# Layer norm and last logits of the second half moved behind the first gather list, shifts and products of ones put into waits, in a gated recurrence, long filter and mixture-of-experts kernel

## The reference, cut to what matters

```python
x = layernorm(h).reshape(-1, D)
gate_logits = x @ gate_weight.T                      # 16 experts
top_vals, top_idx = jax.lax.top_k(gate_logits, 2)
mask = any(top_idx[:, :, None] == arange(E), axis=1)
hs = silu(einsum('td,efd->tef', x, w1))
h_mean = einsum('tef,te->ef', hs, mask) / maximum(counts, 1)[:, None]
y_mean = einsum('ef,edf->ed', h_mean, w2)
out = einsum('tk,tkd->td', softmax(top_vals), y_mean[top_idx])
```

## Time and profile before

| | |
|---|---|
| time, median of 3 runs | 421.78 us (421.72 to 421.83) |
| span of the profiled execution | 501.4 us |
| the profiled execution's own time | the page gives none beside the span |
| instructions | 7310 |
| TensorE busy | 397.6 us, 79% |
| VectorE busy | 311.4 us, 62% |
| ScalarE busy | 218.1 us, 43% |
| GpSimd busy | 205.3 us, 41% |
| granted TensorE clock, mean | 0.877 |
| front, to the last added filter output | 0 to 158.7 us |
| routing | 158.7 to 252.0 us |
| experts | 252.0 to 467.6 us |
| tail | 467.6 to 501.4 us |

### The profile page before, as it was taken

How to read it: one execution, slowest core, us unless ns; L and a number is a source line. 1 busy time by engine, 2 the same in 40 slices (tenths; PEclk the granted TensorE clock), 3 DMA queues, 4 the chain that set the end, 5 groups by cost and what they waited for, 6 DMA issues and landing times.

```text
span 501.4 us, 7310 instructions
## 1 busy us (share of the span) xinstructions
PE 397.6 (79%) x1929; PEld 269.9 (54%) x1930; DVE 311.4 (62%) x827; ACT 218.1 (43%) x423; POOL 205.3 (41%) x231
## 2 busy tenths in 40 slices
PE   8999999998898987554591404589987877899984
PEld 7888888886898974423440101244433433344552
DVE  3598888888788999543530101577744543577884
ACT  3334555445232666536350101456644443567320
POOL 2011111115400998757467775400066666610510
PEclk9999999998998996756587556799999788999998
DMA  6206533322209350647312111100291111100029
GB/s 182 66 1 164 139 86 109 102 80 82 81 1 262 98 140 2 193 140 212 106 57 52 54 52 43 31 0 2 54 331 47 37 47 42 47 16 1 1 73 251
DMA packets 53020, 43.68 MB, mean 87 GB/s; under 512 B 20686, under 2 KB 45980, under 8 KB 52732
## 3 DMA queue, kind: packets, MB, share of 16 engines
q1 hardware_dynamic: 44276, 32.09, 22.3%
q0 software_dynamic: 4416, 9.05, 6.5%
q10 hardware_dynamic: 4296, 2.15, 1.6%
HBM read 34.86 MB, written 8.42 MB: 86 GB/s over the span
## 4 chain that ended last, share of the span: by engine, by line
PE 47%; DVE 19%; issue 12%; another core or an unknown queue 10%; ACT 6%; POOL 3%; DVEq 2%; ACTq 0%; POOLq 0%
PE P L662 16%; PE P L935 14%; PE P L867 6%; ACT P L1265 4%; DVE BIG L1712 3%; DVE H L1828 2%; PE P L905 2%; PE P L1062 2%; PE P L697 2%; PE P L655 1%; POOL XN L597 1%; DVE arena L1504 1%; POOL arena L594 1%; PE P L688 1%
## 5 line engine op out<-in xcount | busy, mean ns | idle before, releaser
L1712 DVE TENSOR_TENSOR BIG<-BIG,P 128x512 f32 x138 | 95.0, 688 | 115.9 <-issue 75.1
L935 PE MATMUL P<-w1T,arena 128*128 x276 | 142.4, 652 | 12.0 <-DVE BIG L1712 8.7
L935 PEld LDWEIGHTS P<-w1T,arena 128*128 128x128 f32 x276 | 52.6, 209 | 67.1 <-issue 66.4
L1254 ACT COPY arena<-P 128x384 f32<-128x384 f32 (+1 forms) x48 | 22.4, 467 | 119.6 <-remote 50.4
L1265 ACT ACTIVATE P<-P 128x512 f32<-128x512 f32 x138 | 72.8, 580 | 1.6 <-PE P L935 1.5
L614 POOL DMA_INDIRECT XN<-table,arena x60 | 58.1, 968 | 30.1 <-issue 18.1
L614 POOL DMA_INDIRECT arena<-table,arena x42 | 39.7, 946 | 57.9 <-PE P L935 40.8
L557 POOL TENSOR_TENSOR rs<-ve,mhalf 123x4 f32<-123x4 f32 x16 | 17.6, 1098 | 101.9 <-DVE ve L1356 101.9
L1103 ACT ACTIVATE arena<-P 128x492 f32<-128x492 f32 x48 | 27.9, 583 | 50.6 <-PE P L662 50.5
L614 POOL DMA_INDIRECT BIG<-table,arena x36 | 34.6, 960 | 24.7 <-remote 12.4
L905 PE MATMUL P<-ident,XN 128*128 128x128 f32 x60 | 11.4, 304 | 41.6 <-issue 35.3
(11 more groups left out here) (242 smaller groups left out, 639.7 us busy)
## 6 DMA issues: line engine op xcount, KB each, us to landing
arena<-kpad SPq DMA_DIRECT2D x16, 492.0 KB, 4.0
XN<-in_L_ffn_w SPq DMA_DIRECT2D x1, 4096.0 KB
arena<-in_x SPq DMA_DIRECT2D x16, 224.0 KB
table<-XN SPq DMA_DIRECT2D x4, 896.0 KB
BIG<-table SPq DMA_DIRECT2D x1, 2048.0 KB
out<-H SPq DMA_DIRECT2D x8, 224.0 KB
out<-H ACTq DMA_DIRECT2D x8, 224.0 KB
BIG<-table SPq DMA_DIRECT2D x1, 1024.0 KB
```

The source lines that it names most:

```text
L935: mm = nc.tensor.matmul(bank[:, :], stat, w1T[:, bass.ds(e * FF, FF)], start=True, stop=True)
L1254: nc.scalar.copy(GTs[:, bank, 0:count * SLOT], PT[:, 0:count * SLOT]).then_inc(GT_ready, 1)
L1712: v.tensor_tensor(at, at, bank[:, :], ALU.add).then_inc(esum_step, 1)
```

## The change

- Statistics of quarters 2 and 3, their moments and shifts, go from in and around the first two searches to `top2(2)` and behind `top2(3)`. Shifts 0 and 1 are made between steps of `top2(0)`.
- Only 13 of the 16 tiles of logits stand before the first list; the last three, and five w1 groups instead of six, stand behind it on TensorE and ScalarE.
- `ranks(3)` stands ahead of `pick_transposes(2)` and w1 10 and 11; `tile_experts(2)` ahead of w1 12 to 15.
- The powers of quarters 2 and 3 stand in the stream of gathers, ahead of numbers 7 and 19. GpSimd norms 8 sequences of quarters 0 and 1 only, VectorE 6 of quarter 3, ScalarE the rest: 4 of quarter 1 and all 16 of quarter 2 between steps of the one-hots, 10 of quarter 3 behind the last w1 copy.
- 89 products of ones (`stay_warm`), of 256 columns in quarters 0 and 1 and 512 in 2 and 3, stand ahead of TensorE's waits. Their results are not read.

```diff
-NORM_POOL = (8, 8, 8, 0)
+NORM_POOL = (8, 8, 0, 0)
+NORM_DVE = (0, 0, 0, 6)
+X2_FIRST = 13
+        RSTD_AT = (7, 19)
...
             clear(7, 8, 16)
             write_table(2)
             clear(11, 0, 4)
-            write_table(3)
             clear(13, 4, 6)
             clear(15, 6, 8)
+            write_table(3)
...
-            norms(0)
+            rstd_of(0)
...
+            rstd_of(1)
+            norms(0)
             norms(1)
-            norms(2)
-            norms(3)
...
+                    if n in RSTD_AT:
+                        rstd_of(QA + RSTD_AT.index(n))
                     if n in paces:
                         pool.wait_ge(*paces[n])
                     gather(n, g)
...
+            def stay_warm(n, wide=False):
+
+                place = P[1][:, :] if wide else P[3][:, 256:512]
+                cols = oneb[:].unsqueeze(1).to_broadcast([128, 4 if wide else 2, 128])
+                for _ in range(n):
+                    nc.tensor.matmul(place, oneb[:], cols, start=True, stop=True)
...
             def ranks(q):
+                stay_warm((0, 4, 2, 1)[q], q >= 2)
...
             def picks(q):
+                    if n == ON_ACT - OG:
+                        stay_warm(3 if q < 2 else 1, q >= 2)
...
             def bit_transposes(q):
+                stay_warm((5, 6, 8, 4)[q], q >= 2)
             def matches(q):
+                stay_warm((4, 3, 1, 5)[q], q >= 2)
...
+                    if a == 2 and q == 0:
+                        tile_base(1)
+                    if a == 2 and q != 2:
+                        stay_warm(3 if q == 3 else 5, q == 3)
...
             def pick_transposes(q):
+                stay_warm(2 if q >= 2 else 4, q >= 2)
...
...
-            for n in range(2 * NHB):
+            for n in range(X2_FIRST):
                 x2_transposes(n)
-                if n == 11:
+                if n == 10:
                     ranks(0)
...
-            for m in range(0, 2):
-                w1_transposes(m)
             bit_transposes(0)
-            tile_base(1)
...
             tile_experts(1, NA)
-            for m in range(2, 8):
+            for n in range(X2_FIRST, 2 * NHB):
+                x2_transposes(n)
+                if n > X2_FIRST:
+                    logits(n - 1)
+            logits(2 * NHB - 1)
+            for m in range(0, 5):
                 w1_transposes(m)
             ranks(2)
-            for m in range(8, 10):
+            for m in range(5, 10):
                 w1_transposes(m)
             bit_transposes(2)
             matches(2)
             picks(2)
+            ranks(3)
             pick_transposes(2)
             for m in range(10, 12):
                 w1_transposes(m)
-            ranks(3)
...
             picks(3)
             pick_transposes(3)
+            tile_experts(2, NB)
             for m in range(12, E):
                 w1_transposes(m)
...
             copy_V(0)
+            for b in NORM_ACT[1][4:]:
+                norm2(b)
...
             for m in range(12, E):
                 copy_w1T(m)
+            for b in NORM_ACT[3]:
+                norm2(b)
             copy_of(0)
...
-            top2(2, nothing)
+            top2(2, more_stats(2))
...
             counts(2)
+            moments2(2)
             experts_of_tiles(1, 0, NA)
...
             top2(3, between)
             counts(3)
+            for b in range(3 * QB, 3 * QB + 6):
+                bn(b)
             places(3)
             placed(2)
             low_onehots(3, 0)
+            for b in range(3 * QB + 6, 4 * QB):
+                bn(b)
+            moments2(3)
...
+            shift(3)
             experts_of_tiles(2, NA, NB)
             placed(3)
+            for b in range(4 * QB - NORM_DVE[3], 4 * QB):
+                a = v.tensor_scalar(XN[0:T, b], H[0:T, b], mm2[0:T, 0, b:b + 1], rs2[0:T, b:b + 1],
+                                    ALU.subtract, ALU.mult)
+            a.then_inc(xn2_dve, 1)
             index_list(2, P[7], NA, NB)
```

More of the change, by code:

```diff
@@ L43 @@
 QW = QB * E
-NORM_POOL = (8, 8, 8, 0)
-NORM_ACT = [list(range(q * QB, (q + 1) * QB - NORM_POOL[q])) for q in range(NQ)]
+NORM_POOL = (8, 8, 0, 0)
+NORM_DVE = (0, 0, 0, 6)
+NORM_ACT = [list(range(q * QB, (q + 1) * QB - NORM_POOL[q] - NORM_DVE[q])) for q in range(NQ)]
 NCHUNK = 2 * NQ
+X2_FIRST = 13
 SLOT = 128
@@ L302, in build @@
         W1_AT, MATCH_AT = {}, {}
-        at_ring = 2 * NHB
-        for part, q in ((range(0, 2), 0), ((), 1), (range(2, 10), 2), (range(10, 12), 3)):
+        X2_AT = list(range(X2_FIRST))
+        at_ring = X2_FIRST
+        for part, q in (((), 0), ((), 1), (range(0, 10), 2), (range(10, 12), 3)):
+            if q == 2:
+                X2_AT += range(at_ring, at_ring + 2 * NHB - X2_FIRST)
+                at_ring += 2 * NHB - X2_FIRST
             for m in part:
@@ L589, in _, with rstd_of @@
             nc.gpsimd.tensor_scalar(rankb[:], rank_in, 1.0, None, ALU.mult).then_inc(pool_const, 1)
-            def norms(g):
+            def rstd_of(g):
                 pool.wait_ge(ve2_ready, g + 1)
@@ L594, in norms @@
                 nc.gpsimd.tensor_tensor(rs2[0:T, qb], ve2[0:T, qb], mhalf[0:T], ALU.pow).then_inc(rstd2, 1)
+            def norms(g):
                 pool.wait_ge(rstd2, g + 1)
@@ L709, in x2_transposes @@
             def x2_transposes(n):
-                if n >= 2:
-                    pe.wait_ge(ring_read, n - 1)
+                at = X2_AT[n]
+                if at >= 2:
+                    pe.wait_ge(ring_read, at - 1)
                 for q in range(4):
-                    mm = nc.tensor.transpose(PR[n % 2][:, q * T:(q + 1) * T], H[0:T, 4 * n + q], ident[0:T, 0:T])
+                    mm = nc.tensor.transpose(PR[at % 2][:, q * T:(q + 1) * T], H[0:T, 4 * n + q], ident[0:T, 0:T])
                 mm.then_inc(ring_mm, 1)
@@ L882, in tile_base @@
             def tile_base(nth):
+                if nth == 2:
+                    stay_warm(4, True)
                 pe.wait_ge(tiles_ready, nth)
@@ L962, in _ @@
             totals(1, 2 * QA)
-            logits(2 * NHB - 1)
+            logits(X2_FIRST - 1)
             pe.wait_ge(match_ok, 1)
-            for m in range(0, 2):
-                w1_transposes(m)
             bit_transposes(0)
-            tile_base(1)
             matches(0)
@@ L1232, in _ @@
                 copy_x2T(n)
-            for n in range(12, 16):
-                if n == 14:
-                    code_OH(0)
-                for b in NORM_ACT[1][2 * (n - 12):2 * (n - 11)]:
-                    norm2(b)
-                copy_x2T(n)
+            copy_x2T(12)
+            code_OH(0)
+            for b in NORM_ACT[1][:4]:
+                norm2(b)
             code_OH(1)
-            for m in range(0, 2):
-                copy_w1T(m)
             copy_bits(0)
@@ L1247, in _ @@
             copy_V(1)
-            for b in NORM_ACT[2]:
-                norm2(b)
-            for m in range(2, 8):
+            for n in range(X2_FIRST, 2 * NHB):
+                copy_x2T(n)
+            for m in range(0, 5):
                 copy_w1T(m)
@@ L1278, in silus_past @@
                         nc.scalar.copy(xh[:, h, 0:4 * T], PRT[:, 0:4 * T]).then_inc(RT_high, 1)
-            for b in NORM_ACT[3][:6]:
-                norm2(b)
             code_OH(2)
-            for m in range(8, 10):
+            for m in range(5, 10):
                 copy_w1T(m)
@@ L1287, in _ @@
             low_onehots(2)
+            for b in NORM_ACT[2][:2]:
+                norm2(b)
             copy_V(2)
+            code_OH(3)
             for m in range(10, 12):
                 copy_w1T(m)
-            for b in NORM_ACT[3][6:]:
-                norm2(b)
-            code_OH(3)
             copy_bits(3)
             low_onehots(3)
+            for b in NORM_ACT[2][2:8]:
+                norm2(b)
             copy_V(3)
+            for b in NORM_ACT[2][8:]:
+                norm2(b)
             for m in range(12, E):
                 copy_w1T(m)
+            for b in NORM_ACT[3]:
+                norm2(b)
             copy_of(0)
@@ L1622, in _ @@
             moments2(1)
-            shift(0)
             def more_stats(g):
@@ L1630, in more_stats, with shifts @@
                 return between
-            top2(0, more_stats(2))
-            for b in range(2 * QB + (4 * 11 + 2) // 3, 3 * QB):
-                bn(b)
-            counts(0)
-            moments2(2)
-            shift(1)
+            def shifts(i):
+                if i in (2, 8):
+                    shift(i // 8)
+            top2(0, shifts)
             def tile_counts(nth):
@@ L1722, in add_tile, with count_first @@
                 accumulate(n, expert_bank(n), n)
-            top2(1, more_stats(3))
-            for b in range(3 * QB + (4 * 11 + 2) // 3, 4 * QB):
-                bn(b)
+            def count_first(i):
+                if i == 2:
+                    counts(0)
+            top2(1, count_first)
             counts(1)
-            moments2(3)
             places(0)
@@ L1733, in _ @@
```

(11 more changed lines are left out.)

17 lines of the change are left out of this document (12 added, 5 removed).

## The result

The changed kernel takes **427.47 us** (median of 4 runs, 426.4 to 428.0) against 421.75 for the kernel before: a ratio of **1.0141, 95% interval 1.0127 to 1.0155**. It is slower by 5.7 us. The forecast was 419.1 in a range up to 424.0, so it missed in sign and in size. The mechanism of case D, a late gather 32, is what happened; its price was put at 1.9 to 3.2.

The account below looks back on a forecast made before the run. Without holds, TensorE's products and the gathers were taken to bound the kernel equally within 1 us. TensorE's chain gains 5.0, the gathers' 2.7 if the runs have the 4.6 us hold: 421.78 - 2.7 = 419.1 us, range 415.0 to 424.0.

Parts of the forecast that it names:

- case D: Rival, slower: the power ahead of gather 19 makes gather 32 late; +1.9, up to +3.2 us, 423.7; chance 0.31.
- 246.0: GpSimd, kernel before: start of gather 32 if the runs too have the 4.6 us hold in VectorE's routing work.
- 243.3: GpSimd, changed kernel: start of gather 32, last moments at 223.9 plus 19.4 for the second power and thirteen gathers.
- VectorE and TensorE up to the lists: Routing stage: first list 4.1 us earlier, quarter 3's counts 6.2 earlier, first expert product 3.2 earlier, at 238.0.
- Number 32 waits for the second list: GpSimd, kernel before: gather 32 starts only once the second list is there, at 252.21 in the profile.
- 241.4: GpSimd, kernel before: start of gather 32 with the holds taken out of the profiled 252.21.
- About 3.5 us lost that nobody waits for: GpSimd's gather stream: the first power, ahead of gather 7, loses about 3.5 us at no cost to the end.
- 237.1, then 1 to issue and 4 to land: 242: SyncE: second table write, behind ScalarE's last norm at 237.1, lands at 242, when gather 32 may start.
- A: Forecast chosen: the gathers set the end and start 2.7 us earlier, 419.1 us; chance 0.32.
- the equality of the two chains: Expert stage, kernel before: TensorE's products and the gathers end within 1 us of each other, so both must be shortened.
- 415.8: Kernel before: span in us without holds, 501.4 less 74.8, 6.2 and 4.6; the median was 421.78.
- B: Rival: TensorE sets the end and gathers keep up, needing an interval under about 1.17 us; -5.0 us, 416.8; chance 0.20.

Follow-up runs that it names:

- split wait: Changed kernel, table writes of quarters 2 and 3 on semaphores of their own, gather 32 waiting for quarter 2's alone, 42 for quarter 3's: 424.43 us, 1.0077 to before.
- the profiled TensorE experiment: Kernel before with eight products of ones on TensorE right ahead of the first expert product: 421.48 us, ratio 1.0009 to before.

## Why the prediction was wrong

The forecast of -2.7 us was the start of gather 32 moving from 246.0 to 243.3. It measured 242.15 before and 247.45 after: 3.9 us from the old start and 4.1 from the new one, 8.0 of the 8.4 between the forecast and the 5.7 measured.

The stream of gathers in GpSimd's queue accounts for the loss. After minus before, between fixed gathers (before from the profile of its schedule with products ahead of the experts, which has no long hold):

| piece | before | after | difference |
|---|---|---|---|
| start of gather 0 | 199.90 | 194.86 | -5.04 |
| gather 0 to 6 | 7.78 | 7.93 | +0.15 |
| gather 6 to 7, first power | 1.25 | 4.84 | +3.59 |
| gather 7 to 19, second power | 15.89 | 19.15 | +3.26 |
| gather 19 to 31 | 16.09 | 15.34 | -0.75 |
| gather 31 to 32, the write | 1.24 | 5.33 | +4.09 |
| gather 32 to 137 | 132.74 | 133.24 | +0.50 |
| start of gather 137 | 374.89 | 380.69 | +5.80 |

+5.80 in the last gather, +5.76 in the last product, and 5.7 in the medians. Point by point:

- **VectorE and TensorE up to the lists: right in the times.** First gather near 195.9 (194.86), counts of quarter 3 at 215.0 (214.67), last moments at 223.9 (223.17), first product at 238.0 (237.26); the clock was 1.00 between 184 and 200; the wait at L1687 is gone and that at L1568, 4.82 in the kernel before without holds, is 1.25; the ten norms stand right before the first copy. Two things were wrong and cost nothing at the end. The first group was to be warm (2.9 us) and ran at half clock (4.70 to the second one, as before). And the w1 groups ran at full clock, where I had them cold at 0.86; the row behind that figure has 20 transposes, five groups and not six. Between 200 and 212 the clock is 1.00 with the change and 0.98 without the products of ones, and in both the logits' products stand right ahead of these groups; that they brought it up was not tried.
- **"Number 32 waits for the second list": the step that failed first.** I took a wait of 3.02 us out of an execution with 75 us of holds, in which all that GpSimd waits for was late, and moved the holds, not the wait. Without holds there is no wait: gather 32 of the kernel before starts at 242.15, and 32 intervals behind the first gather put it there, not the list. The number 241.4 was near by luck, the reason wrong, and the reason decides what a power costs. It also decides the old start that the forecast used. The codes of the second list, which number 32 waits for by its pace, are done on TensorE at 238.2 in that profile, 4.0 ahead of gather 32; so even a hold of 4.6 there would have moved it by less than 1 us, and not to 246.0, and the profile has no such hold.
- **"About 3.5 us lost that nobody waits for": wrong.** Somebody waits for each microsecond of a full stream. Both powers cost 6.9 us by the table and 6.2 by the run without them, more than the 5.0 that the earlier list gave. The forecast 243.3 for gather 32 holds without the write (243.38, and 243.32 with the split wait), because the moments (223.17) come just as GpSimd's turn does (223.65). Against 242.15 that is +1.2.
- **"237.1, then 1 to issue and 4 to land: 242": the mis-sized term.** Gather 32 starts on the write's landing at 247.45, 11.4 us behind the last norm (236.07). I named SyncE's queue in the diff but didn't add it up: the three clears (2 MB) are issued from 231.15 on and stand ahead of the write; quarter 2's write, issued at 206 in the kernel before and at 229 now, stands right ahead of them. The write was to land at 242 and so to add nothing behind 243.3; it added 4.1, all of the 3.8 by which D's 1.9 missed 5.7. That the wait for this write costs it is shown (split wait: the last gather 3.9 earlier); that what stands ahead in the queue makes the write late is shown for 1.7 of it (two clears taken from ahead), and the rest is not divided.
- **The choice of A over D: wrong.** It rested on the equality of the two chains, which TensorE's slack of 1.4 us or more speaks against, and on 6.0 us between 415.8 and the median, read as holds that the runs might have too. 1.74 of them lie around the span, in this run and in that of the profiled TensorE experiment (421.64 for a span of 419.9). The other 4.1 are what I had taken out too much. The Trainium skill ("Runtime: NRT & Kernel Launch", "The ~15µs preamble/postamble breakdown") has a gap of some 6.2 us in which the profile's total is the longer of the two. Here the execution's time is longer than the span, by 1.74, so that figure does not explain the 6.0; that the case it was taken to speak for, D, came was luck.
- **B's bound was right.** Outside holds 130 of the 137 intervals are 1.24 to 1.26 and the other seven longer, so gathers could not keep up with TensorE.

The loss is thus shown, not only argued: split wait -3.9 us in the last gather, powers out -6.2 in the length of the stream, and with both gone the rest of the change, its early start above all, is worth 3.3 to 4.3 us (0.9921 and 0.9898).

## What to carry to other kernels

Before an operation goes into an engine's queue, add up that queue alone from its first to its last instruction: if it never waits, everything put into it costs its full time, however idle the data it works on. Add up the DMA queue in the same way, in bytes ahead of the transfer that somebody waits for, and let each wait name only the part that it needs. And from an execution with long holds take durations, never waits: a wait that ends in a hold may not exist without it.

## What the runs showed of the hardware that was not expected

- A write of 984 KB from XN to the table (896 KB and 88 KB) needed 8.9 us from its issue at 236.90 to gather 32 behind 1 MB of clear, 10.2 when it was issued 2 us earlier (234.89 to 245.05), and 11.4 us from ScalarE's last norm to gather 32 behind 2 MB.
- Eight fp32 products of 128x128 ones took 2.02 us ahead of the first expert product, 0.25 each.
- The new function on ScalarE cost one table load of 1.28 us and 0.21 for 123x16.
- In the nine profiles with the change's order up to the first list and its products of ones, the first gather starts anywhere from 194.70 to 197.21. The two latest (196.13 and 197.21) belong to executions that were the slowest of their kernel.
